# Graph attention: the residual scaled and added by VectorE straight from PSUM

## The reference, cut to what matters

```python
Wh1 = h @ W[:IN_C];  Wh2 = h @ W[IN_C:]          # h is the normalised x
s1 = Wh1 @ a_w;      s2 = Wh2 @ a_w
e = s1[:, None] + s2[None, :] + a_b
e = jnp.where(e >= 0, e, ALPHA * e)
e = jnp.where(adj > 0, e, NEG_BIG)
att = jax.nn.softmax(e, axis=1)
return att @ (h @ fc_w + fc_b)
...
x = x + _L0_gnn_ref(_layernorm(x, axis=-1), adj, ...)
```

## Time and the profile before

| | before |
|---|---|
| median of 3 runs | 1169.57 us (1167.49 to 1171.04) |
| the profiled execution | 1167.08 us, its span 1165.3 us |
| TensorE busy | 1032.5 us, 89% of the span |
| VectorE busy | 757.0 us, 65% |
| ScalarE busy | 618.3 us, 53% |
| GpSimd busy | 446.8 us, 38% |
| granted TensorE clock, mean over the span | 0.949 of full speed |
| attention, steady state | about 104 to 347 us of the span |
| last statistics of the attention end | 383.39 us |

### The profile page before, as it was taken

How to read it: one execution, slowest core, us unless ns; L and a number is a source line. 1 busy time by engine, 2 the same in 40 slices (tenths; PEclk the granted TensorE clock), 3 DMA queues, 4 the chain that set the end, 5 groups by cost and what they waited for, 6 DMA issues and landing times. The chain is left out here.

```text
span 1165.3 us, 23845 instructions
## 1 busy us (share of the span) xinstructions
PE 1032.5 (89%) x7616; PEld 823.2 (71%) x7617; DVE 757.0 (65%) x1598; ACT 618.3 (53%) x948; POOL 446.8 (38%) x363
## 2 busy tenths in 40 slices
PE   6639999999999599898987999996499999999991
PEld 5538989898989589687754888885266666666661
DVE  3799999999992464855675566666355455454550
ACT  1677888888873577767642112221145454454441
POOL 0244666666662000019140134453134444444443
PEclk9969999999999599899999999998699999999996
DMA  9998777777710311220053799998323333333322
GB/s 379 191 299 270 228 248 230 245 229 244 235 50 1 112 73 63 83 73 1 1 118 81 187 246 225 256 245 298 117 46 46 54 51 48 54 46 54 51 40 23
DMA packets 72587, 161.49 MB, mean 139 GB/s; under 512 B 7504, under 2 KB 58448, under 8 KB 66512
## 3 DMA queue, kind: packets, MB, share of 16 engines
q1 hardware_dynamic: 48656, 97.59, 26.9%
q0 software_dynamic: 18128, 40.17, 19.6%
q10 hardware_dynamic: 5744, 22.94, 5.5%
HBM read 137.34 MB, written 45.49 MB: 157 GB/s over the span
## 5 line engine op out<-in xcount | busy, mean ns | idle before, releaser
L554 PE MATMUL PS<-G,PT 128*128 128x256 f16 x2028 | 233.6, 273 | 0.0
L554 PEld LDWEIGHTS PS<-G,PT 128*128 128x128 f16 x2028 | 198.4, 98 | 22.1
L1576 PE MATMUL PS<-W,X 128*128 x708 | 165.5, 384 | 8.6 <-DVE X L1732 6.6
L1576 PEld LDWEIGHTS PS<-W,X 128*128 128x128 f16 x708 | 69.5, 98 | 97.0 <-issue 31.7
L1502 PE MATMUL PS<-own_H,adj_room 128*128 128x256 f16 x572 | 129.3, 272 | 0.0
L1500 PE MATMUL PS<-own_H,adj_room 128*128 128x257 f16 x572 | 129.3, 273 | 0.0
L1822 POOL DMA_INDIRECT out_dram<-X,place_i x59 | 92.2, 1563 | 88.4 <-DVE place_i L1746 80.6
L420 DVE SCALAR_TENSOR_TENSOR score<-S2low,S1low,S2row 128x3327 f32<-128x3327 f32 x26 | 114.5, 4405 | 1.4 <-ACT S2low L299 1.4
L538 PE MATMUL PS<-ident,probs 128*128 128x128 f32 x676 | 90.5, 280 | 26.0 <-ACT probs L327 16.8
L1596 PE MATMUL PS<-adj_room,X 128*128 x472 | 111.6, 380 | 0.3 <-issue 0.3
L426 DVE CUSTOM_DVE_ANT_0 score<-score,maskbias 128x3327 f32<-128x3327 f32 x26 | 100.0, 3848 | 6.2 <-DVE score L420 6.0
(11 more groups left out here) (273 smaller groups left out, 1991.8 us busy)
## 6 DMA issues: line engine op xcount, KB each, us to landing
adjf<-adj_dram SPq DMA_DIRECT2D x26, 1664.0 KB, 8.0
slot_rows<-blank SPq DMA_DIRECT2D x26, 1032.0 KB, 10.9
adj_room<-adjT_dram POOLq DMA_DIRECT2D x22, 832.0 KB, 9.8
W<-eW_dram ACTq DMA_DIRECT2D x8, 1024.0 KB, 4.8
adj_room<-eW_dram ACTq DMA_DIRECT2D x8, 1024.0 KB, 9.1
X<-slot_rows SPq DMA_DIRECT2D x59, 129.0 KB, 3.3
own_H<-eb_dram SPq DMA_DIRECT2D x8, 512.0 KB, 5.2
adj_room<-eW_dram ACTq DMA_DIRECT2D x8, 512.0 KB, 7.5
```

The lines of the kernel that those rows point to most:

```text
L554: mm = nc.tensor.matmul(acc[u][:, 0:D], left, right, start=(j == 0 and n == 0), stop=(j == T - 1 and n == 2))
L1576: mm = nc.tensor.matmul(psHE[u][:, n * F1:(n + 1) * F1], left[u][:, k, :], W1[:, e, k, part, n * F1:(n + 1) * F1], start=(m == 0), stop=(m ...
```

## The change

ScalarE's scaled copy (`weigh`) and GpSimd's addition (`residual`) are left out, with the buffer `attended`. VectorE gets one operation per tile in their place: it reads `acc` from PSUM, multiplies it by `rscale`, adds `X` and writes `X`. It stands between the masking of tile t + 2 and the low half of group 0 of tile t. Waits for `weighed` become waits for `x_ready`, and the wait for the bias DMAs moves from GpSimd to VectorE, ahead of its loop.

```diff
-            def residual(t, u):
-                if isinstance(t, int) and t == 0:
-                    pool.wait_ge(fcb_added, 16 * len(XG))
-                settled(pool, add_waits, (weighed, t + 1))
-                nc.gpsimd.tensor_tensor(X[:, t, :], X[:, t, :], attended[u][:, :], ALU.add).then_inc(x_ready, 1)
...
-                if live(t - 2):
-                    residual(t - 2, u)
...
-            def weigh(t, u):
-                settled(act, exp_waits, (acc_ready, t + 1), (scale_ready, t + 1), (x_ready, t - 1))
-                nc.scalar.activation(attended[u][:, :], acc[u][:, 0:D], ACT.Copy,
-                                     scale=rscale[u][:, :]).then_inc(weighed, 1)
...
-                if live(t - 2):
-                    weigh(t - 2, u)
...
             def row_scale(t, u):
                 dve.wait_ge(inverted, t + 1)
-                wait(dve, weighed, t - 1)
+                wait(dve, x_ready, t - 1)
                 v.tensor_scalar(rscale[u][:, :], rtotal[u][:, :], g_back[:, :], None, ALU.mult).then_inc(scale_ready, 1)
+
+            def residual(t, u):
+                dve.wait_ge(acc_ready, t + 1)
+                dve.wait_ge(scale_ready, t + 1)
+                v.scalar_tensor_tensor(X[:, t, :], acc[u][:, 0:D], rscale[u][:, :], X[:, t, :], ALU.mult,
+                                       ALU.add).then_inc(x_ready, 1)
...
                 if live(t + 2):
                     masked(t + 2, u)
+                if live(t - 2):
+                    residual(t - 2, u)
                 if live(t):
                     lo(t, u, 0)
...
+            dve.wait_ge(fcb_added, 16 * len(XG))
             steps(dve, iteration, FIRST, LAST, TOTAL)
...
                 if g == 0:
-                    wait(pe, weighed, t - 1)
+                    wait(pe, x_ready, t - 1)
```

More of the change, by code:

```diff
@@ L179, in attention @@
         rowmax, shift_by, total, rtotal, rscale = (small(n) for n in ("rowmax", "shift_by", "total", "rtotal", "rscale"))
-        attended = [sb(f"attended{u}", [P, D]) for u in range(2)]
         blank = sb("blank", [P, ROW])
```

## The result

| | before | after |
|---|---|---|
| median of 19 runs each | 1169.77 us | 1165.71 us (1158.38 to 1169.21) |
| ratio after to before, 95% interval | | 0.9957 (0.9941 to 0.9973) |
| span of the profiled execution | 1165.3 us | 1156.6 us |
| first score's start to last statistics' end | 327.58 us | 325.28 us |
| TensorE's time for a pair of tiles, mean | 23.22 us | 23.07 us |

The change makes the kernel 0.43% faster, 4 to 5 us. The last two rows of the table compare what the change touches: the attention from VectorE's first score on. It gave 2.30 us, where 3.3 us were predicted. Of the 8.7 us between the spans, 1.7 us lie ahead of the first score (54.11 against 55.81 us, before anything that was edited runs), 2.3 us in this stretch and 4.7 us behind it.

A forecast was written before the change was run, and what follows sets the result against it. A two-tile loop through four engines was taken as the bound: -0.36 - 0.28 + 0.40 = -0.24 us per pair, 11 times 2.64, plus 0.68 at the end, 3.3 us: 1169.57 to 1166.3 us, range 1162.6 to 1170.3.

The forecast's parts named there:

- The forecast of 1166.3 us: Whole kernel: 3.3 us saved from the median of 1169.57 us, all in the attention stage; chance 0.60.
- The bound: Attention's steady state: a closed loop over two tiles through TensorE, ScalarE, GpSimd and VectorE sets the pace, 23.22 us.
- Rival D: VectorE bounds the attention: each tile from the third on gets 0.40 us more, 1177.7 us; chance 0.10.
- Step 1: ScalarE's scaled copy leaves the loop between exponential and raw copy, so GpSimd's cast comes earlier: -0.36 us per pair.
- Step 2: GpSimd's addition goes and no longer holds up VectorE between the subtraction's end and the low half: -0.28 us per pair.
- Step 3: VectorE's new operation lies inside the loop, between masking and low half: +0.40 us per pair.
- rival C: New operation costs its upper bound: each pair loses 0.02 us, the end gains 0.42, 1169.4 us; chance 0.15.
- Step 4: Waits: x_ready is never last, and the bias DMAs land by 62.7 us, before VectorE's loop near 74.5 us.
- Step 5: Attention stage's end: last statistics finish 1.16 us after TensorE's release, at 382.71 us, 0.68 us earlier.
- Rival B: TensorE becomes the bound at 22.74 us per pair, so the gain stops at 6.0 us, 1163.6 us; chance 0.12.
- Rival E: VectorE's score starts before GpSimd's subtraction, which is stuck, then the masking: 15.4 us slower, 1185.0 us; chance 0.03.
- The later stages are taken as unchanged: Stages behind the attention: simply start earlier, with no gain or loss of their own.

The follow-up runs named there:

- late: Changed kernel with VectorE's residual moved behind the low half of group 0 and the inversion; stage 321.56 us, ratio to before 0.9921, repeated 0.9919.
- twice: Changed kernel with a second operation of the same form ahead of each residual, its result unread; stage 329.99 us, ratio to before 1.0009.
- unroll6: Changed kernel with VectorE's loop unrolled six tiles instead of two; stage 324.52 us, ratio to before 0.9947.
- late6: Changed kernel with the edits of late and of unroll6 together; stage 321.55 us, ratio to before 0.9932.
- add_to_vector: Kernel before with only GpSimd's addition moved to VectorE, ScalarE still making the scaled copy; stage 328.81 us, ratio to before 1.0000.
- padded: Changed kernel with one more VectorE operation of about 2.3 us behind the last statistics, its result unread; 1167.86 us, ratio to before 0.9989.

## Why the prediction was right, and where not

- **The forecast of 1166.3 us** met a median of 1165.71 us, inside the range, and the direction was right. But the closeness is partly luck: 3.3 us were forecast for the attention, which gave 2.3, and some 2 us were gained elsewhere, where none were forecast.
- **The bound** (a loop over two tiles through four engines, not VectorE's busy share) was right. It is shown by late (same work, 3.8 us less in the stage) and by twice (0.40 us per pair, not per tile). Rival D, slower by VectorE's sum, fell with that: scores went from 4535 to 4235 ns, as they had been waiting for GpSimd. (Its price counted the 22 tiles of 11 pairs; from the third on there are 24, which makes 1178.5 us and changes nothing.) The first half of the rule in the Trainium skill's "Perfetto Trace Analysis" ("Optimizing Scalar/DVE Operations"), that work may be moved away from a saturated VectorE, did not help at this place: VectorE counts as busy for 235.6 of the 241 us from 104 to 345 us in the changed kernel's profile (98%, blocked time included), it took on an instruction, and the stage grew shorter. Its second half, that GpSimd and VectorE share a read port, fits the 0.29 and 0.11 us by which GpSimd's addition had held the masking up.
- **Step 1**, ScalarE's copy, -0.36: right. The cast comes 7.13 us after the transposes, 0.43 sooner. The other 0.07 us come from the change of tile: ScalarE's high half waits 0.81 us in the tile that now closes the loop (starting 1.07 us after the transposes), 0.88 us in the one that closed it before (1.15). I read this as ScalarE's own way back, since the tiles written out ahead of and behind its loop have 0.81 too; its loop was not unrolled, so that is argued and not tested.
- **Step 2**, GpSimd's addition, -0.28 per pair: right for the loop that closed before, mis-sized for the pair. In the kernel before the tile that closes the loop has no way back in front of its masking, and the addition holds the masking up for 0.28 us:

```profile
178.90 3.90 DVE L426 CUSTOM_DVE_ANT_0 score<-score,maskbias 128x3327 f32<-128x3327 f32 x1 [0.17 <-DVE score L420]
```

  The tile that now closes it is the one that holds VectorE's way back, and there only 0.11 us came free. The prediction followed one loop and took the other for no slower. From subtraction to low half it is 7.78 us: 7.49 - 0.28 + 0.40 + 0.17. (On the other tile it is 7.62, where 7.61 was forecast.) The pair's sum is then -0.43 - 0.28 + 0.40 + 0.17 = -0.14 us (23.22 to 23.08), not -0.24. By the means, 23.217 to 23.066, 11 times 0.15 is 1.7 us.
- **Step 3**, the new operation, +0.40: right (169.26 - 168.86), with a duration of 480 ns and no gap in front of it, so rival C is out. Neither it nor GpSimd slowed the other. Its place in the loop was priced rightly too: late took it out and gained up to TensorE's own pace.
- **Step 4**, the waits: from 108 to 346 us no engine waited for x_ready. The bias DMAs held nothing up that shows beyond 0.1 us: one masking, at 72.90 us, has 0.28 us in front of it where it had 0.18.
- **Step 5**, the end, -0.68: it was -0.70 (1.84 to 1.14 us).
- **Rival B** (TensorE the bound) didn't come, it takes late to get there, with 6.0 us from the stage, as B was priced. Its floor was set slightly too high, at 22.74 us; late shows 22.71. **Rival E**, the flip, didn't come: the subtraction takes 2.13 us throughout.
- **"The later stages are taken as unchanged"** is the step that the timings don't bear out. In all seven timed comparisons of kernels whose attention ends earlier (after three times, late twice, unroll6, late6) the timed gain exceeds the attention's by 1.6 to 4.0 us: for late 0.0079 x 1168 = 9.2 us against 6.0. One such excess could be chance, given the intervals; seven of the same sign hardly, even though those on one chip share the runs of the kernel before. It doesn't need an attention that ends earlier, either: twice, 2.4 us longer there, is timed only 1.0 us slower, and add_to_vector, 1.2 us longer, not slower at all, and in both the stage's difference lies just outside the timed interval. The short drops of TensorE's clock behind the attention differ between these kernels, but no run shows that they are the cause: the window shown doesn't follow the gain, and padded was too coarse to show it. This stays open.

The version to keep is late: 0.9921 (0.9905 to 0.9938) and 0.9919 (0.9897 to 0.9941) against before, where the change itself has 0.9957, 0.9967 and 0.9946.

## What to carry to other kernels

Before pricing a moved operation, close the loop: follow one stop of the busiest engine back through every engine until it comes round, and check that the pieces add up to the measured period. Then an operation costs its time only if it lies in that loop, and the cheapest gain may be to move it a few lines down. Take the reference for a piece from the same kind of iteration: a loop's way back, a written-out first tile or the other buffer can differ by as much as the term that is being worked out.

## What the runs showed of the hardware

- A hardware loop's way back costs about 0.17 us on VectorE (0.35 against 0.18 us in front of the masking, once in six tiles with unroll=6). On ScalarE every second tile of the loop has 0.88 us against 0.81 us in front of the high half, which looks like the same thing and was not tested. In the kernel before VectorE's was invisible in the time, since GpSimd's addition held the same instruction up anyway.
- VectorE's score, with two inputs in SBUF, is not slowed in proportion by GpSimd: it lasts its own 3.67 us plus what is left of GpSimd's subtraction at its start, less 0.18 to 0.20 us. At 160.53 the subtraction has 0.95 us left, and the score takes 4.43.
- One kernel, the one before, had medians of 1168.2 to 1169.8 us in three of the four comparisons and of 1160.1 us on the chip of the fourth; the profile of 1158.1 us from there spends 296.4 us between first and last write of the final stage, where the first profile has 299.9 (and the changed kernel's first one 299.5).
